# Attention and MoE low-rank FFN on 8 cores: both heads' scores in three shared PSUM banks, a third rotating bank, next pair's K and Q ahead of its last V tiles, low-rank transposes later

## What is computed

```python
# x: [1, 8192, 2048]
q, k, v = x @ Wq, x @ Wk, x @ Wv                  # 32 heads of 64
scores = q @ k.T * 64 ** -0.5 + dog_bias          # blocks of 512 queries, 1024 keys
scores = where((dist >= 0) & (dist < 512), scores, -1e30)
m = maximum(scores.max(-1), sink)
p = exp(scores - m)
out = (p @ v) / (p.sum(-1) + exp(sink - m))
x = layernorm(x + out @ Wo)
w = normalised top-2 of softmax(x @ router_w.T)   # 8 experts
Ax = x @ lora_A                                   # rank 16 for each expert
x = layernorm(x + x @ weight.T + 2 * (Ax * w) @ lora_B)
```

## Time and profile before

| | us |
|---|---|
| median of 3 runs (lowest, highest) | 957.73 (957.59, 958.37) |
| the profiled execution, whole | 958.39 |
| its slowest core, first to last instruction | 956.4 |
| its fastest core | 952.7 |
| PE busy in the slowest core | 880.1 (92%) |
| DVE busy | 539.0 (56%) |
| ACT busy | 426.5 (45%) |

### The profile page before, as it was taken

How to read it: one execution, slowest core, us unless ns; L and a number is a source line. 1 busy time by engine, 2 the same in 40 slices (tenths; PEclk the granted TensorE clock), 3 DMA queues, 4 the chain that set the end, 5 groups by cost and what they waited for, 6 DMA issues and landing times.

```text
span 956.4 us, 18656 instructions; the slowest of 8 cores (952.7 to 956.4 us)
## 1 busy us (share of the span) xinstructions
PE 880.1 (92%) x6440; PEld 496.8 (52%) x6440; DVE 539.0 (56%) x1623; ACT 426.5 (45%) x927; POOL 36.4 (4%) x73
## 2 busy tenths in 40 slices
PE   3588999999999999999999999999999999997995
PEld 0345566456646645655664664565444455454442
DVE  1034566566565665656566566656775636636544
ACT  2034555566556655556555565656530332131000
POOL 3000000000000000000000000000000000000000
PEclk9889999999999999999999999999999999999998
DMA  8998625764352361443335134231979486002212
GB/s 132 156 167 139 97 43 95 128 100 81 59 94 33 68 113 23 95 72 68 72 68 94 13 84 101 38 94 24 183 148 204 105 145 120 1 1 110 90 66 88
DMA packets 22027, 86.37 MB, mean 90 GB/s; under 512 B 2672, under 2 KB 2672, under 8 KB 18864
## 3 DMA queue, kind: packets, MB, share of 16 engines
q0 software_dynamic: 9504, 53.51, 32.2%
q1 hardware_dynamic: 12432, 31.68, 14.8%
HBM read 125.91 MB, written 8.59 MB: 141 GB/s over the span
## 4 chain that ended last, share of the span: by engine, by line
PE 82%; DMA 8%; DVE 5%; issue 3%; ACT 1%; POOL 0%; DVEq 0%; ACTq 0%; POOLq 0%
PE psP L356 16%; PE psP L385 16%; PE psP L369 12%; DMA sb<-xt 8%; PE psT L457 7%; PE psS L617 7%; PE psS L504 5%; PE psP L504 5%; PE psS L405 5%; PE psP L617 4%; PE psP L484 3%; DVE sb L493 1%; PE psT L564 1%; DVE sb L525 1%; DVE sb L531 1%
## 5 line engine op out<-in xcount | busy, mean ns | idle before, releaser
L439 ACT ACTIVATE sb<-sb 128x641 bf16<-128x641 f32 x256 | 211.9, 828 | 148.8 <-DVE sb L428 146.4
L428 DVE CUSTOM_DVE_ANT_0 sb<-psS,sb 128x641 f32<-128x641 f32 (+4 forms) x256 | 171.4, 689 | 121.6 <-PE psS L405 101.5
L356 PE MATMUL psP<-sb 128*128 128x512 bf16 x768 | 189.0, 386 | 24.1 <-DMA sb<-xt 24.1
L385 PE MATMUL psP<-sb 128*128 128x256 bf16 x1536 | 188.7, 276 | 18.0 <-DVE sb L493 13.9
L385 PEld LDWEIGHTS psP<-sb 128*128 128x128 bf16 x1536 | 145.0, 99 | 49.9 <-issue 33.1
L421 DVE CUSTOM_DVE_ANT_0 sb<-psS,sb 128x512 f32<-128x512 f32 (+3 forms) x128 | 62.6, 489 | 129.1 <-PE psS L405 129.1
L369 PE MATMUL psP<-sb 128*128 128x512 bf16 x512 | 123.3, 385 | 2.6 <-DMA sb<-wq 2.6
L356 PEld LDWEIGHTS psP<-sb 128*128 128x128 bf16 x768 | 68.5, 98 | 106.8 <-issue 42.7
L451 DVE TENSOR_SCALAR sb<-sb 128x640 bf16<-128x640 bf16 x256 | 87.3, 383 | 13.7
L457 PEld LDWEIGHTS psT<-sb 128*128 128x128 bf16 x1280 | 82.4, 98 | 21.7 <-issue 1.4
L457 PE MATMUL psT<-sb 128*128 128x128 bf16 x1280 | 92.9, 220 | 0.5 <-DVE sb L451 0.5
(11 more groups left out here) (100 smaller groups left out, 615.2 us busy)
## 6 DMA issues: line engine op xcount, KB each, us to landing
sb<-gscr SPq DMA_DIRECT2D x32, 320.0 KB, 6.7
sb<-wk POOLq DMA_DIRECT2D x16, 512.0 KB, 6.3
sb<-wv POOLq DMA_DIRECT2D x8, 1024.0 KB, 10.4
sb<-wq POOLq DMA_DIRECT2D x16, 512.0 KB, 6.2
sb<-gscr SPq DMA_DIRECT2D x32, 256.0 KB, 7.2
sb<-wo POOLq DMA_DIRECT2D x4, 2048.0 KB, 26.5
sb<-wt POOLq DMA_DIRECT2D x4, 2048.0 KB, 16.7
y<-sb SPq DMA_DIRECT2D x16, 512.0 KB, 3.2
```

The source lines that it names most:

```text
L356: tok = put("T", lambda t, i=i: t.matmul(bank_ap(bank, [1, 512]), b(WK[pr % 2] + i * 128, [1, 128]), b(XT[blk] + i * 512, [1, 512]), start ...
L385: tok = put("T", lambda t, i=i: t.matmul(bank_ap(bank, [1, 256]), b(XT[blk] + i * 512 + part * 128, [1, 128]), b(WV[g % 2] + i * 256, [1, ...
L428: ttr_last[pr] = ttr_tok[u, hh] = put("V", lambda v: v.tensor_tensor_reduce(out=f(sx + 2 * halo, [1, 641 - halo]), in0=p(psS[hh], halo, [1 ...
L439: e_tok[u, hh] = put("S", lambda s: s.activation(b(PB[u % 3 * 2 + hh], [1, 641]), f(SX[u % 2 * 2 + hh], [1, 641]), ACT.Exp, bias=f(st + 4 ...
```

## The change

- `psP` has three banks that rotate. `psS` is one tensor of three banks for both heads: head 0 from column 0, head 1 from column 768. The middle bank (columns 512 to 1023) holds the last 128 scores of head 0 and the first 256 of head 1.
- `scores(u)` is still four matmuls: head 0 with 512 columns, head 1 with 256, head 1 with 384, head 0 with 128. The last one has a wait of PE on its own semaphore (`own=shared`), until the 256-column one is finished, so that the two row halves never write the middle bank together. The first waits for the `bias_min` of both heads of step u-1, and `bias_min` of either head waits for the last matmul.
- `window_work`: in even pairs K and Q of the next pair stand ahead of the last four V tiles. `load_wv`, and two loads of residual rows, are issued three steps later.
- In pair 15 two partial output groups are fed instead of four.
- `scx_transpose` of tiles 0 to 3 stands behind all four `ffn_main`, and that of tiles 4 to 7 two or three groups later.

The diff, whose cut hunk only puts `psS` with `HEAD[hh]` for `psS[hh]`, and `s_tok[u]` for `s_tok[u, hh]`:

```diff
--- before.py
+++ after.py
@@ -38,7 +38,7 @@
         self.waited = {e: {} for e in "TVSGY"}
         self.turn = {"Y": 0, "G": 0}
 
-    def put(self, eng, fn, after=(), mark=False, dma=False):
+    def put(self, eng, fn, after=(), mark=False, dma=False, own=None):
         after = [t for t in after if t is not None]
         signal = None
         if dma:
@@ -53,7 +53,7 @@
             sem = ENGINE_SEM[eng]
             self.value[sem] += 1
             signal = (sem, 1)
-        waits = []
+        waits = [own] if own else []
         for s, v in after:
             if eng == "T" and s == "sT":
                 continue
@@ -184,13 +184,14 @@
         return bass.AP(sf, row * NF + off // 2, [[NF, rows]] + [list(d) for d in dims])
 
     ctx = contextlib.ExitStack()
-    psP = [ctx.enter_context(nc.psum_tensor(f"psP{i}", [128, 512], F32)) for i in range(2)]
+    psP = [ctx.enter_context(nc.psum_tensor(f"psP{i}", [128, 512], F32)) for i in range(3)]
     psT = [ctx.enter_context(nc.psum_tensor(f"psT{i}", [128, 1024], BF16)) for i in range(2)]
-    psS = [ctx.enter_context(nc.psum_tensor(f"psS{i}", [128, 1024], F32)) for i in range(2)]
+    psS = ctx.enter_context(nc.psum_tensor("psS", [128, 1536], F32))
+    HEAD = (0, 768)
     sems = {s: ctx.enter_context(nc.semaphore(s)) for s in ALL_SEMS}
 
     def p(t, off, *dims, row=0, rows=128):
-        pitch = 512 if t is psP[0] or t is psP[1] else 1024
+        pitch = 1536 if t is psS else 1024 if t is psT[0] or t is psT[1] else 512
         return bass.AP(t, row * pitch + off, [[pitch, rows]] + [list(d) for d in dims])
 
     plan = Plan()
@@ -308,7 +309,7 @@
     t_g = [put("Y", lambda y, k=k: y.dma_start(
         out=bass.AP(g_dram, k * 32 * GW, [[GW, 32], [1, GW]]), in_=row([GG, GH][k])),
         after=[t_gh], dma=True) for k in range(2)]
-    t_pz = [vop(lambda v, k=k: v.memset(p(psS[k], 640, [1, 1]), 0.0)) for k in range(2)]
+    t_pz = [vop(lambda v, k=k: v.memset(p(psS, HEAD[k] + 640, [1, 1]), 0.0)) for k in range(2)]
 
     bias_tok, halo_tok = {}, {}
     ttr_last, ttr_halo_last, sink_tok = {}, {}, {}
@@ -331,8 +332,8 @@
     load_bias(0)
 
     banks = list(psP)
-    bank_free = dict.fromkeys(range(2))
-    bank_ready = collections.deque(range(2))
+    bank_free = dict.fromkeys(range(3))
+    bank_ready = collections.deque(range(3))
 
     def next_bank():
         k = bank_ready.popleft()
@@ -399,17 +400,20 @@
     def scores(u):
         pr, n, c = steps[u]
         tile = n * 4 + c
-        for part in range(2):
-            for hh in range(2):
-                c0, w = ((0, 512), (512, 128))[part]
-                s_tok[u, hh] = put("T", lambda t, hh=hh, c0=c0, w=w: t.matmul(
-                    p(psS[hh], c0, [1, w]),
-                    b(QT[pr % 2] + tile * 128, [1, 128], row=64 * hh, rows=64),
-                    b(KT[pr % 2] + tile * 128 + c0, [1, w], row=64 * hh, rows=64),
-                    start=True, stop=True, tile_position=(64 * hh, 0)),
-                    after=[k_tok[pr, n], k_tok[pr, n + 1], q_tok[pr, n], t_pz[hh],
-                           ttr_tok.get((u - 1, hh))], mark=(part == 1))
-        s_last[pr] = s_tok[u, 1]
+        shared = None
+        for hh, c0, w in ((0, 0, 512), (1, 0, 256), (1, 256, 384), (0, 512, 128)):
+            tok = put("T", lambda t, hh=hh, c0=c0, w=w: t.matmul(
+                p(psS, HEAD[hh] + c0, [1, w]),
+                b(QT[pr % 2] + tile * 128, [1, 128], row=64 * hh, rows=64),
+                b(KT[pr % 2] + tile * 128 + c0, [1, w], row=64 * hh, rows=64),
+                start=True, stop=True, tile_position=(64 * hh, 0)),
+                after=[k_tok[pr, n], k_tok[pr, n + 1], q_tok[pr, n], t_pz[0], t_pz[1],
+                       ttr_tok.get((u - 1, 0)), ttr_tok.get((u - 1, 1))],
+                mark=(w < 300), own=shared if w == 128 else None)
+            if w == 256:
+                shared = tok
+        s_tok[u] = tok
+        s_last[pr] = tok
 
     def bias_min(u, hh):
         pr, n, c = steps[u]
@@ -419,17 +423,17 @@
-                out=f(sx, [1, halo]), in0=p(psS[hh], 0, [1, halo]),
+                out=f(sx, [1, halo]), in0=p(psS, HEAD[hh], [1, halo]),
-                after=[s_tok[u, hh], halo_tok[pr, hh], e_tok.get((u - 2, hh))], mark=True)
+                after=[s_tok[u], halo_tok[pr, hh], e_tok.get((u - 2, hh))], mark=True)
...
@@ -676,21 +680,23 @@
             k_or_q("k", 1, 1)
         k_or_q("k", pr, 2)
         k_or_q("q", pr, 1)
-        if pr % 2 == 0:
-            v_tiles(pr // 2, range(8, 12) if pr == 0 else range(6, 12))
+        if pr and pr % 2 == 0:
+            v_tiles(pr // 2, range(6, 8))
         if pr + 1 < NPAIR:
             if pr:
                 k_or_q("k", pr + 1, 0)
                 k_or_q("k", pr + 1, 1)
             k_or_q("q", pr + 1, 0)
-        if pr % 2 == 1 and pr // 2 + 1 < 8:
+        if pr % 2 == 0:
+            v_tiles(pr // 2, range(8, 12))
+        elif pr // 2 + 1 < 8:
             v_tiles(pr // 2 + 1, range(6))
         if pr == 15:
             for t, oc in EARLY:
                 feed.add(("w", t, oc), wo_group(t, oc, 0, NI - 1))
 
-    EARLY = [(0, 0), (1, 0), (2, 0), (0, 1)]
-    LATER = [(3, 0), (1, 1), (2, 1), (3, 1)]
+    EARLY = [(0, 0), (1, 0)]
+    LATER = [(2, 0), (3, 0)]
 
     pending_pv = collections.deque()
 
@@ -703,7 +709,7 @@
                 for (t, oc), (t2, oc2) in zip(LATER, EARLY):
                     feed.add(("w", t, oc), wo_group(t, oc))
                     feed.add(("w", t2, oc2), wo_group(t2, oc2, NI - 1, NI))
-                for oc in (2, 3):
+                for oc in (1, 2, 3):
                     for t in range(4):
                         feed.add(("w", t, oc), wo_group(t, oc))
 
@@ -744,17 +750,19 @@
         feed.run(quota * 0.5)
         if n == 0 and c == 0 and pr + 1 < NPAIR:
             load_bias(pr + 1)
+        if n == 0 and c == 2 and pr % 2 == 1:
+            if pr // 2 + 2 < 8:
+                load_wv(pr // 2 + 2)
+            if pr == 13:
+                load_r(0, "G", [wv_done[6]])
+            if pr == 15:
+                load_r(2, "G", [wv_done[7]])
         if n == 1 and c == 3:
-            if pr % 2 == 0 and pr // 2 + 2 < 8:
-                load_wv(pr // 2 + 2)
             if pr == 2:
                 load_wo(0)
-            if pr == 12:
-                load_r(0, "G", [wv_done[6]])
             if pr == 14:
                 feed.until([("k", 15, 0), ("k", 15, 1), ("q", 15, 0)])
                 load_wo(1, [wk_done[15], wv_done[7]])
-                load_r(2, "G", [wv_done[7]])
                 load_wo(2, [wq_done[15], wv_done[7]])
 
     normalise(U)
@@ -773,9 +781,9 @@
     late_tok[0] = at_tok[15, 1]
     for k in range(2):
         t_rep[k] = vop(lambda v, k=k: v.memset(f(RTS[k] + 32, [1, 8]), HUGE), *late)
-    for i in range(4):
-        banks.append((psS[i // 2], 512 * (i % 2)))
-        release(2 + i, ttr_tok[U, i // 2])
+    for i in range(3):
+        banks.append((psS, 512 * i))
+        release(3 + i, ttr_tok[U, 1])
     feed.drain()
 
     y_cast(0)
@@ -796,6 +804,7 @@
     held = []
     for t in range(4):
         held.append((t, 0) + ffn_main(t, 0))
+    for t in range(4):
         scx_transpose(t)
     for h in held:
         ffn_low(*h)
@@ -808,11 +817,13 @@
                 y_transpose(4 + (idx - 1) // 2, (idx - 1) % 2)
             if idx in (8, 9, 10, 11):
                 router(4 + idx - 8)
-            if idx in (9, 10, 11, 12):
-                scx_transpose(4 + idx - 9)
+            if idx in (11, 12):
+                scx_transpose(4 + idx - 11)
     for t in range(4, 8):
         for oc in range(4):
             ffn_low(t, oc, *ffn_main(t, oc))
+            if t == 4 and oc < 2:
+                scx_transpose(6 + oc)
 
     def finish_all(y):
         ins = None
```

More of the change, by code:

```diff
@@ L428, in bias_min @@
         ttr_last[pr] = ttr_tok[u, hh] = put("V", lambda v: v.tensor_tensor_reduce(
-            out=f(sx + 2 * halo, [1, 641 - halo]), in0=p(psS[hh], halo, [1, 641 - halo]),
+            out=f(sx + 2 * halo, [1, 641 - halo]), in0=p(psS, HEAD[hh] + halo, [1, 641 - halo]),
             in1=f(BI[pr % 2][hh] + 2 * halo, [1, 641 - halo]), scale=1.0, scalar=init,
             op0=ALU.add, op1=ALU.min, accum_out=f(st + 4 * hh + 2, [1, 1])),
-            after=[s_tok[u, hh], bias_tok[pr, hh], sink_tok[pr, hh], first,
+            after=[s_tok[u], bias_tok[pr, hh], sink_tok[pr, hh], first,
                    e_tok.get((u - 2, hh))], mark=True)
```

## The result

| | before | changed |
|---|---|---|
| median of the executions | 957.88 us | 972.64 us |
| ratio to before, 95% interval | | 1.0149 [1.0129, 1.0169] |
| profiled execution, whole and its slowest core | 958.4, 956.4 us | 971.0, 969.4 us |
| spans of the eight cores | 952.7 to 956.4 us | 964.7 to 969.4 us |

The changed kernel is slower by 1.5%, 14.3 us by the ratio; the forecast was 8.

A forecast was written before the change was run, and what follows sets the result against it. PE, busy 92% of the span with 82% of the chain, was taken as the bound. 37.2 + 4.8 - 14.6 - 0.3 - 9.0 - 9.7 = +8.4 us gave 965.8 us against the median; range 958.5 to 971.5.

The forecast's parts named there:

- Low-rank transposes: FFN: moved later, the transposes lose their four PE waits, at most 0.3 us left at the longest; -9.7 us net.
- Scores: the added wait: Each step's scores: PE's wait for itself makes 0.68 us of 0.38, 0.30 in 124 steps; +37.2 us.
- order of issue: Scores: the 256-column matmul reports not before the 512-column one issued ahead of it, at 0.39 us; the central assumption.
- own length: Rival, scores: the 256-column matmul reports at 0.28 us, a step costs 0.19, total 952.5 us, faster; chance 0.08.
- Third bank: PV between two V tiles: the next tile no longer waits for PV's own bank; -14.6 us, a fifteenth wait 0.3.
- the third bank does nothing: Rival: PV's successor waits for ACT or DVE all the same; +14.6, 980 us; chance 0.02.
- K and Q first: Start of odd pairs: scores no longer wait for the Q copy, 1.12 us in eight pairs; -9.0 us.
- Pair 15: Last pair: unfed steps, moved matmuls +4.1, clock drop +1.5, output groups' waits -0.8; together +4.8 us.
- the gains fall short: Rival: DVE's FFN chain sets the transposes' time or pair 15's clock stays low; half of 9.7 lost, 970.7; chance 0.08.

The follow-up runs named there:

- e1_short_first: The changed kernel with head 1's 256-column score matmul issued ahead of head 0's 512-column one; ratio to the kernel before 0.9985.
- e11_v_last: The changed kernel with the V tiles and the two kinds of loads where they were before; ratio to the kernel before 1.0249.
- e5_early4: The changed kernel with four early output groups in pair 15 again and residual tile 2 loaded between the weight loads; ratio to the kernel before 1.0098.
- e7_late_only: The kernel before with the later low-rank transposes alone; 955.3 us, ratio to the kernel before 0.9951.

## Why the prediction was wrong

The direction was right, and by the mechanism named for it; the size was too small by 5.9 us (14.3 against 8.4) and the time lies outside the range. The step that failed is **Low-rank transposes**: the term of -9.7 measured -4.7 to -5.4, since a wait of 2.2 us for ACT's copy was left where the step has at most 0.3, and 1.6 us of its saving stood on the slowest core alone. Most other terms were off by 1 to 2 us, in both directions.

- *Scores: the added wait, +37.2.* Right in kind: `e1_short_first` decides between order of issue and own length, and the rival "own length" is false. The step is 0.69 instead of 0.68. At 0.311 x 124 the term is 38.6, 1.4 too small. My 0.39 for the report was 0.41; the 0.15 and 0.14 behind it measured 0.135 and 0.145.
- *Third bank, -14.6 - 0.3.* All 15 waits are gone, so the rival "the third bank does nothing" is false. In steps 8 to 119, 112 own waits of 0.311 are 34.8. `e11_v_last` has these and the bank, in the old order, and its stretch is +22.0: beside the kernel before the bank gave 12.8, and I had 14.9. (The 16 above are beside a kernel that has the late starts as well.) I had missed that the new order adds seven such collisions, which the bank hides as well; it doesn't move the sum, but it makes each of the two changes look worse alone.
- *K and Q first, -9.0.* By `e11_v_last` 1.0% or 9.6 us. In steps 8 to 119 it is 9.0, where seven of my eight waits are 7.8. The errors of this term and of the bank's are opposite, and together they are 21.7 against my 22.7.
- *Pair 15, +4.8.* The stretch is +5.5, of which five own waits are 1.6: about 4.0. From scores 124 to scores 127 it is 0.1 shorter than before (I had 0.4, the clock's 1.5 included). Thirty more matmuls than before stand behind the last PV, and from that PV to `y_transpose` it is 5.88 longer (28 moved matmuls at 6.0 in my sum, less 0.8). The piece in between is 1.0 shorter, which I hadn't counted. The 4.9 of `e5_early4` are the price of the two groups fewer in this kernel, and not this term, which counts from the kernel before.
- *Low-rank transposes, -9.7.* By `e7_late_only` 4.7, by the stretch 5.4. The sentence that fails is "so a wait of at most 0.3 is left". I followed the transpose on PE and DVE, and not its copy, which ACT makes and which stands behind operations that wait for DVE: 2.2 to 2.3 us. The other part is 3.0 us of wait and 1.7 of clock, read on core 1: there the part up to the low-rank matmul is 1.6 longer than on the others, since elsewhere the clock's drop was absorbed by the wait behind it. Up to that matmul the two make up the whole shortfall of tiles 4 to 7 (8.9 expected, 5.1 measured). The end of the FFN behind it is some 0.5 longer than before, and why is open. The rival "the gains fall short" had this outcome, half of the 9.7 lost, and its 970.7 is near the time; the reason that I gave it, DVE's chain, was only half the reason, as ACT is what stands between.

By the stretches the terms are 38.6 for the own waits, -12.8 and -9.0 for bank and order in steps 8 to 119, -1.3 for the two before step 8, +4.0 and -5.4: together 14.1, where I had 8.4. That they close is no proof, since some are what a stretch leaves once the own waits are taken off. Of the 5.7 between the sums 4.3 are the low-rank transposes, 1.4 the own waits and 2.1 the bank, and order and pair 15 take back 2.1. That these other errors partly cancel, to 1.4, is luck: with that one term right I would have had 970.1 us, still about 2 short of the measured time.

## What to carry to other kernels

When two matmuls in different row halves run side by side and something waits for the shorter, issue the shorter first and make it as short as the layout allows: here the order moved the step from 0.69 to 0.57 us, which took the change back to the time before, and the shorter piece to 0.52, which made it a gain (0.9919). When a step is moved later, follow its result through every engine up to its reader, and ask on each in-order queue what now stands ahead of it; for a saving read on the slowest core, look at the same wait on another core first. Before you read a short idle time as a cost, look whether it is there on a core that has all its records. Price a reordering and a buffer together: here the order was worth next to nothing with two banks and 9 us with three.

## What the runs showed of the hardware

- A 256-column matmul reported 0.41 us after its start behind a 512-column one in the other half of the rows, and at 0.29 when issued ahead of it.
- A 130-column matmul issued first reported at 0.24 us.
- When PE waits for its own semaphore, about 0.135 us pass from the increment to the start of the waiting matmul (0.409 to 0.544 us, 0.294 to 0.429, 0.242 to 0.377).
- With two rotating banks and that wait, 40 to 48 of 112 steps had the next work start up to 0.24 us later still, 3.7 to 4.4 us together; with three banks 9 to 18 steps did. Why is open.
- A fall of the granted clock to half for 3.4 us cost about 1.5 us on cores where no wait for another engine came after it (30.9 to 31.1 us against 29.5), and nothing where one did: those cores took the same 29.5 us as cores without a fall.
